# TensorE alternates the two layers of neighbouring expert turns, and GpSimd makes 21 more small gathers, in a graph and expert network kernel

## The chip, the cores and the metric

The kernel runs on one core of a Trainium2 chip. The metric is the device time of one execution in microseconds (us), lower is better. Before the change it is 1894.84 us, the median of three runs (1893.95 to 1897.71).

## The reference, cut to what matters

A layernorm of 6250 nodes x 256 features feeds a graph attention layer over 100,000 edges and a linear attention; their sum is the input of a mixture of experts. Only the last part bears on the change:

```python
logits = xt @ Wr + br                      # 8 experts
top_p, top_idx = jax.lax.top_k(softmax(logits), 2)
weights = top_p / top_p.sum(axis=-1, keepdims=True)
xn = (xt - mu) * jax.lax.rsqrt(var + LN_EPS)
xe = xn * ln_g[e] + ln_b[e]
h = gelu(xe @ W1[e] + b1[e])               # 256 -> 1024, exact gelu
y = h @ W2[e] + b2[e]                      # 1024 -> 256
out = x + sum over the two chosen experts of weight * y
```

## The kernel before

The program is written out by hand for each engine; semaphores order the engines against each other, and each engine works through its own queue in order. It has these stages: the table of node features; a walk over the edges in 196 groups of 512, for which GpSimd gathers rows of the table (784 indirect DMAs, line 843) while the two attention layers are finished beside it; the router, in which VectorE finds each token's two experts and its place; and the expert stage, which is the change's place.

In the expert stage the 12,500 pairs of token and expert are sorted into blocks of 128 rows, each block owned by one expert. There are 57 **turns**: 48 of two blocks (256 rows, "double" below) and 9 of one block (128 rows, "single"). `place_of` sets their order: three doubles, then nine times five doubles and a single, so the singles are turns 8, 14, 20 and so on to 56, the last. `subs_of(s)` is 1 for a single.

A turn `s` goes through the engines like this:

- GpSimd gathers the rows (`get_rows`, line 893) up to five turns ahead, and the gates (`get_gates`, line 898).
- TensorE transposes the rows (`pe_turn_rows`, line 2279); VectorE scales them (`dve_affine`, line 1932), ScalarE casts the high half and VectorE makes the low half (lines 1206 and 1937).
- TensorE computes the first layer, `pe_up` (line 2294): 8 parts `f` of six matmuls, each with a moving operand as wide as the turn has rows. The expert is a number in memory: `expert_at` (line 549) loads it into a register, and the addresses of the weights are worked out from it by register instructions between the matmuls, two `k` by two halves of the weights for a part.
- ScalarE takes the gelu of each two parts (`act_tile`, line 1183), VectorE splits it into two halves (lines 1951 and 1952).
- TensorE computes the second layer, `pe_down` (line 2315): 8 parts of six matmuls for a double and three for a single, all with a moving operand of 256 columns. It may start when VectorE has read the banks of the turn before (`y_ready`).
- VectorE adds the bias (`dve_answer`, line 1966), ScalarE multiplies by the gate (`act_gate`, line 1197), and GpSimd adds the block to the output (`add_rows`, line 907), one block after the other: each add waits until the one before it has landed.

TensorE's own order is in `pe_tile`: in turn `s` it transposes the rows of turn `s + 1`, then does the first layer of turn `s`, then the second layer of turn `s - 1`. VectorE's turn `s` (`dve_tile`) prepares the rows of `s + 1`, then splits the four pairs of parts of `s`, then answers for `s - 1`; the instructions of an engine run in that order.

When all is done, each engine ends with a DRAIN instruction and the program is over.

Of the kernel before, what the change touches and what calls it, by code (L numbers as in the profile page):

```python
# [9 lines left out]
P = 128  # L10
N, D = 6250, 256
# [24 lines left out]
FR = 2 * P  # L36
# [18 lines left out]
AHEAD, GATES_AHEAD = 5, 2  # L55
PARKS = 2 * (X + 1)
# [117 lines left out]
def build(nc, x, src, dst, gnn_w, attn_l, attn_r, gnn_bias, wq, bq, wk, bk, wv, bv, wo, bo,  # L174
          wr, br, ln_g, ln_b, w1, b1, w2, b2, out):
    ctx = ExitStack()
    with ctx:
        ctx.enter_context(nc.allow_non_contiguous_dma(reason="narrow rows of parameters"))

        def sb(name, shape, dt=F32):  # L180
            return ctx.enter_context(nc.sbuf_tensor(name, shape, dt))

        def sem(name):
            return ctx.enter_context(nc.semaphore(name))
# [165 lines left out]
        iota16 = sb("iota16", [P, P], F16)  # L350
        small = region(sb("small", [P, 488])[:, :], 488)
# [30 lines left out]
        tb_few = tables([P, X])  # L382
        wide = region(mid_g[:, :, :].rearrange("p a b -> p (a b)"), RG * D)
# [90 lines left out]
        consts = sem("consts")  # L474
        consts_v = sem("consts_v")
# [307 lines left out]
        def _(pool):  # L783
# [6 lines left out]
            pool.memset(ones16[:, :], 1.0).then_inc(consts, 1)  # L790
            pool.memset(edge_rows[:, 0:7, :], 0).then_inc(pads_set, 1)
# [140 lines left out]

            pool.wait_ge(places_ready, 1)
# [1045 lines left out]
        def _(pe):  # L1979
# [303 lines left out]
            def pe_up(s):  # L2283

                u, rows = s % 2, rows_at(s)
                e = expert_at(pe, s)
                pe.wait_ge(x_turn, 2 * s + 2)
                for f in range(KF):
                    if f % 2 == 0 and s:
                        pe.wait_ge(gelu_ready, 4 * s - 3 + f // 2)  # L2290
                    n = 0
                    for k in range(KD):
                        for wh, xh in ((0, 0), (0, 1), (1, 0)):
                            last = pe.matmul(bank[f // 2][:, (f % 2) * FR:(f % 2) * FR + rows],  # L2294
                                             w1_s[:, bass.ds(e, 1), k, wh, f * P:(f + 1) * P].rearrange("p a b -> p (a b)"),
                                             x_hl[:, u, xh, k, 0:rows], start=n == 0, stop=n == 5)
                            n += 1
                    if f % 2 == 1:
                        last.then_inc(h_made, 1)

            def pe_down(s):
                u = s % 2
                if s == 0:
                    pe.wait_ge(w2_in, X * 16)
                    pe.wait_ge(tau_turn, 1)
                e = expert_at(pe, s)
                if s:
                    pe.wait_ge(y_ready, s)
                for f in range(KF):
                    if f % 2 == 0:  # L2310
                        pe.wait_ge(h_turn, 8 * s + 2 + f)
                    for wh, hhs in ((0, (0, 1)), (1, (0,))):
                        for sub in range(subs_of(s)):
                            for hh in hhs:
                                last = pe.matmul(bank[4 + sub][:, 0:D], h_hl[:, u, hh, f, sub * P:(sub + 1) * P],  # L2315
                                                 w2_s[:, bass.ds(e, 1), f // (KF // 2), wh, f % (KF // 2), :].rearrange("p a b -> p (a b)"),
                                                 start=f == 0 and wh == 0 and hh == 0, stop=f == KF - 1 and wh == 1)
                last.then_inc(y_made, 1)
# [8 lines left out]
            def pe_tile(s):  # L2327
                if s + 1 < FT:
                    pe_turn_rows(s + 1)
                pe_up(s)  # L2330
                if s == 0:
                    pe_unused()
                else:
                    pe_down(s - 1)
# [35 lines left out]
```

## Time and profile before

| | us |
|---|---|
| median of three runs | 1894.84 |
| the profiled execution | 1891.82 |
| its span, first to last instruction | 1890.1 |
| TensorE busy | 1581.7 (84%) |
| VectorE busy | 1368.5 (72%) |
| GpSimd busy | 1218.3 (64%) |
| ScalarE busy | 1079.1 (57%) |

In the profile PE is TensorE's matmuls and PEld its weight loads, which overlap them; DVE is VectorE, ACT ScalarE, POOL GpSimd, SP SyncE. A name with q behind it (PEldq, POOLq) is the engine's instruction sequencer, which works out registers, waits on semaphores and hands work to the engine ahead of its execution. `L2294` is line 2294 of the kernel before. The start of a timeline row is in us from the span's start.

### The profile page before, as it was taken

Reading aid. Unit: us, or ns where it says so; the run is one execution under the profiler, and the core shown is the slowest. Engines: PE = TensorE matmul, PEld = TensorE weight load, DVE = VectorE, ACT = ScalarE, POOL = GpSimd, SP = SyncE. Lnnn points to the kernel's source line nnn. Section 1 sums busy time; section 2 is a strip of 40 time slices with the busy share of each in tenths; the row PEclk is TensorE's granted clock in tenths of the full one; section 3 lists DMA queues with packets and bytes.
Section 4 is the critical chain, followed back from the end, with each engine's and each line's share of the span. In section 5 each row is a group of like instructions: output and inputs, shape, how many; then the busy total and the mean of one; then the engine's idle time right before and its main releaser. Section 6 shows DMA issues by size and latency. Waiting matters only on the chain. (4 is left out here: it accounts for less than half of the span.)

```text
span 1890.1 us, 46784 instructions
## 1 busy us (share of the span) xinstructions
PE 1581.7 (84%) x11358; PEld 1300.0 (69%) x11358; DVE 1368.5 (72%) x3833; ACT 1079.1 (57%) x3043; POOL 1218.3 (64%) x1135
## 2 busy tenths in 40 slices
PE   7858777788787989888887778629999999999995
PEld 5635555455566777777775666517888889888884
DVE  6656567677667888888888999897666656665662
ACT  4655566566666666677666776563444444444441
POOL 2077777777777777777677776105666666666663
PEclk8978899999999999999998888658999999999998
DMA  7745565566544555555555665652333333333332
GB/s 223 247 122 138 168 174 164 165 176 179 150 117 127 155 150 150 141 152 145 142 139 179 183 202 162 200 199 45 53 48 53 49 48 50 53 50 49 46 53 24
DMA packets 149158, 239.37 MB, mean 127 GB/s; under 512 B 27536, under 2 KB 114824, under 8 KB 147624
## 3 DMA queue, kind: packets, MB, share of 16 engines
q0 software_dynamic: 61216, 132.39, 30.4%
q1 hardware_dynamic: 85944, 103.15, 16.8%
q8 instruction: 109, 1.79, 0.4%
q14 instruction: 145, 1.19, 0.2%
q10 hardware_dynamic: 1744, 0.85, 0.2%
HBM read 180.78 MB, written 55.52 MB: 125 GB/s over the span
## 5 line engine op out<-in xcount | busy, mean ns | idle before, releaser
L843 POOL DMA_INDIRECT w_s<-table,w_s x784 | 806.4, 1029 | 279.9 <-issue 231.4
L2092 PE MATMUL bank<-w_s 128*128 128x260 f32 x1952 | 515.9, 410 | 110.3 <-DVE w_s L1536 110.0
L2092 PEld LDWEIGHTS bank<-w_s 128*128 128x128 f32 x1952 | 378.1, 201 | 206.0 <-DVE w_s L1536 139.9
L1026 ACT ACTIVATE w_s<-w_s 128x64 f32 x976 | 260.3, 337 | 68.3 <-ACT w_s L1021 68.1
L1536 DVE SCALAR_TENSOR_TENSOR w_s<-w_s 128x256 f32<-128x256 f32 x732 | 275.7, 426 | 26.7 <-ACT w_s L1026 18.9
L2294 PE MATMUL bank<-acc,w_s 128*128 128x256 f16 (+1 forms) x2736 | 290.4, 265 | 1.6 <-DVE acc L1937 1.5
L2315 PE MATMUL bank<-w_s,acc 128*128 x2520 | 284.5, 273 | 7.2 <-DVE acc L1951 5.5
L907 POOL DMA_INDIRECT out<-mid_g,low_g x105 | 177.2, 1687 | 151.2 <-ACT mid_g L1197 90.6
L2294 PEld LDWEIGHTS bank<-acc,w_s 128*128 x2736 | 252.9, 98 | 30.7 <-issue 2.1
L2315 PEld LDWEIGHTS bank<-w_s,acc 128*128 128x128 f16 x2520 | 245.8, 98 | 37.0 <-issue 8.7
L1033 ACT COPY w_s<-bank 128x512 bf16<-128x512 bf16 x244 | 142.1, 582 | 202.8 <-PE bank L2072 202.3
L1197 ACT ACTIVATE mid_g<-acc 128x256 f32<-128x256 f32 x105 | 48.1, 501 | 276.2 <-DVE acc L1966 217.7
L1183 ACT ACTIVATE acc<-bank,params 128x256 f32<-128x256 f32 (+1 forms) x456 | 174.3, 459 | 31.1 <-PE bank L2294 22.7
L1503 DVE SCALAR_TENSOR_TENSOR w_s<-w_s,iota 128x512 bf16<-128x512 f32 x244 | 181.8, 745 | 1.9 <-issue 0.9
L893 POOL DMA_INDIRECT acc<-xn_d,low_g x105 | 102.6, 977 | 95.9 <-DVEq L1891 63.4
L1952 DVE SCALAR_TENSOR_TENSOR acc<-acc 128x512 f16<-128x512 f32 (+1 forms) x228 | 149.7, 656 | 7.8
L1522 DVE SCALAR_TENSOR_TENSOR w_s<-w_s 128x16 f32<-128x16 f32 x244 | 43.4, 178 | 151.4 <-POOLq L849 148.9
L1015 ACT CAST w_s<-w_s 128x512 f32<-128x512 bf16 x244 | 152.1, 624 | 0.0
L1966 DVE SCALAR_TENSOR_TENSOR acc<-bank,stage 128x256 f32<-128x256 f32 x105 | 40.1, 420 | 140.1 <-PE bank L2315 139.6
L898 POOL DMA_INDIRECT acc<-gate_d,low_g x105 | 111.6, 1063 | 32.0 <-issue 32.0
L2072 PE MATMUL bank<-w_s 128*128 128x128 bf16 x976 | 99.5, 227 | 38.7 <-DVE w_s L1503 37.9
L2072 PEld LDWEIGHTS bank<-w_s 128*128 128x128 bf16 x976 | 75.7, 104 | 79.2 <-DVE w_s L1503 37.4
(308 smaller groups left out, 2187.6 us busy)
## 6 DMA issues: line engine op xcount, KB each, us to landing
stage<-in_L_ffn_W SPq DMA_DIRECT2D x32, 512.0 KB, 4.2
w_s<-table,w_s POOLq DMA_INDIRECT x784
w_s<-in_x SPq DMA_DIRECT2D x48, 256.0 KB, 4.0
w_s<-xT_d SPq DMA_DIRECT2D x96, 128.0 KB
w_park<-low_g SPq DMA_DIRECT2D x18, 512.0 KB
w_s<-w_park SPq DMA_DIRECT2D x9, 1024.0 KB, 9.1
xn_d<-acc SPq DMA_DIRECT2D x7, 896.0 KB, 5.0
table<-w_s SPq DMA_DIRECT2D x24, 260.0 KB, 3.5
```

What stands on the lines that cost most here:

```text
L843: pool.indirect_dma_start(out=ring[:, u, k, :], out_offset=None, in_=table[:, :], in_offset=bass.IndirectOffsetOnAxis(ap=srcT[:, (q * RING ...
L907: pool.indirect_dma_start(out=out[:, :], out_offset=bass.IndirectOffsetOnAxis(ap=add_at[:, column(s, sub):column(s, sub) + 1], axis=0), in ...
L1015: act.copy(hot32[:, k.at % 4, :, :], hot16[:, k.at % 4, :, :]).then_inc(hot32_ready, 1)
L1026: last = act.activation(m[:, e, 0:GD], rows[:, e, 0:GD], ACT.Copy, scale=m[:, e, GD:HC])
L1183: last = act.activation(h32[:, f, 0:n], bank[q][:, (f % 2) * FR:(f % 2) * FR + n], ACT.Gelu, bias=b1T[:, bass.ds(e * KF + f, 1)], scale=UN ...
L1503: dve.scalar_tensor_tensor(hot16[:, k.at % 4, :, :], dstT[:, bass.ds(group * SUB, SUB)].unsqueeze(2).to_broadcast([P, SUB, P]), tile_v[:, ...
L1536: last = dve.scalar_tensor_tensor(m[:, e:e + GH, 0:GD], rows[:, e:e + GH, 0:GD], 1.0, m[:, e:e + GH, GD:HC].to_broadcast([P, GH, GD]), ALU ...
L1952: lambda: dve.scalar_tensor_tensor(h_hl[:, u, 1, f0:f1, 0:n], h32[:, f0:f1, 0:n], ASCALE, h_hl[:, u, 0, f0:f1, 0:n], ALU.mult, ALU.subtract))
L2072: last = pe.transpose(turned16[:, s, :], hot16[:, k.at % 4, s, :], ident16[:, :])
L2092: last = pe.matmul(bank[2 + k.at % 2][:, 0:ROW], hot32[:, k.at % 4, s, :], msg[:, k.at % 2, s, :], start=s == 0, stop=s == SUB - 1)
L2294: last = pe.matmul(bank[f // 2][:, (f % 2) * FR:(f % 2) * FR + rows], w1_s[:, bass.ds(e, 1), k, wh, f * P:(f + 1) * P].rearrange("p a b -> ...
L2315: last = pe.matmul(bank[4 + sub][:, 0:D], h_hl[:, u, hh, f, sub * P:(sub + 1) * P], w2_s[:, bass.ds(e, 1), f // (KF // 2), wh, f % (KF // ...
```

## The change

In a turn of 128 rows TensorE no longer does the first layer of `s` and then the second layer of `s - 1`: it alternates one part of the one with one part of the other (`pe_mixed`). The waits and the load of the expert of both stand at its start. `up_begin` and `down_begin`, which other turns use too, wait first and then load the expert; before, the load came first.

The second part adds `FILL` = 21 indirect gathers on GpSimd, each of 128 rows of 8 numbers from the router's weights at index 0, into a tile that nothing reads. They come after the last addition of the router stage and before the first gather of the expert stage. With the 784 gathers of the walk and 3 x 105 of the expert stage they make 1120, a multiple of 32.

```diff
+LOT = 32
+FILL = -(EC + 3 * COLS) % LOT
...
+        fill_at = sb("fill_at", [P, 1], I32)
...
+        filled = tables([P, FILL, X])
...
+            pool.memset(fill_at[:, :], 0).then_inc(fill_set, 1)
...
+            pool.wait_ge(fill_set, 1)
+            for n in range(FILL):
+                pool.indirect_dma_start(out=filled[:, n, :], out_offset=None, in_=wr[:, :],
+                                        in_offset=bass.IndirectOffsetOnAxis(ap=fill_at[:, :], axis=0)).then_inc(filled_up, 16)
+            pool.wait_ge(filled_up, 16 * FILL)
             pool.wait_ge(places_ready, 1)
...
+            def up_begin(s):
+                pe.wait_ge(x_turn, 2 * s + 2)
+                return expert_at(pe, s)
...
+            def down_begin(s):
                 if s == 0:
                     pe.wait_ge(w2_in, X * 16)
                     pe.wait_ge(tau_turn, 1)
-                e = expert_at(pe, s)
                 if s:
                     pe.wait_ge(y_ready, s)
+                return expert_at(pe, s)
...
+            def pe_mixed(s):
+
+                e_up, e_down = up_begin(s), down_begin(s - 1)
+                for f in range(KF):
+                    up_part(s, e_up, f)
+                    down_part(s - 1, e_down, f)
...
             def pe_tile(s):
                 if s + 1 < FT:
                     pe_turn_rows(s + 1)
-                pe_up(s)
-                if s == 0:
-                    pe_unused()
+                if subs_of(s) == 1:
+                    pe_mixed(s)
                 else:
-                    pe_down(s - 1)
+                    pe_up(s)
+                    if s == 0:
+                        pe_unused()
+                    else:
+                        pe_down(s - 1)
```

`up_part` and `down_part` are the bodies of the loops over `f` of `pe_up` and `pe_down`, unchanged, with their waits on `gelu_ready` and `h_turn`.

TensorE's queue at the start of a single turn, turn 8, in the kernel before (`ISA` is a register instruction, or one of the load's; the bank and tile names lack their numbers; waits stand in brackets):

```order
L2279 MATMUL bank<-ident,acc 128x128 [waits x_turn,rows_got1]
L2279 MATMUL bank<-ident,acc 128x128 x3
L549 TENSOR_LOAD low_g
L549 ISA x2
L2294 ISA [waits gelu_ready,x_turn]
L2294 MATMUL bank<-acc,w_s 128x128 x2
L2294 ISA
L2294 MATMUL bank<-acc,w_s 128x128
```

and the same place now, where line 2290 is the transposes, 554 the load, 2306 the first layer and 2328 the second:

```order
L2290 MATMUL bank<-ident,acc 128x128 [waits x_turn,rows_got1]
L2290 MATMUL bank<-ident,acc 128x128 x3
L554 TENSOR_LOAD low_g [waits x_turn]
L554 ISA x2
L554 TENSOR_LOAD low_g [waits y_ready]
L554 ISA x2
L2306 ISA [waits gelu_ready]
L2306 MATMUL bank<-acc,w_s 128x128 x2
L2306 ISA
L2306 MATMUL bank<-acc,w_s 128x128
```

The wait on `y_ready`, which stood behind the 48 matmuls of the first layer, stands ahead of them now, and the second layer's load of the expert stands behind that wait. The first layer keeps its matmuls and its register instructions; the second layer's come between its parts.

GpSimd's queue at the start of the expert stage before:

```order
L887 TENSOR_TENSOR acc<-acc,w_s 128x7x256 [waits mid_read0,x2_made,elu_made]
L893 DMA acc<-xn_d,low_g 128x256 [waits xn2_out0,xn2_out1,places_ready]
L893 DMA acc<-xn_d,low_g 128x256 x3
```

and now:

```order
L893 TENSOR_TENSOR acc<-acc,w_s 128x7x256 [waits mid_read0,x2_made,elu_made]
L941 DMA low_g<-in_L_ffn_Wr,fill_at 128x8 [waits fill_set]
L941 DMA low_g<-in_L_ffn_Wr,fill_at 128x8 x20
L899 DMA acc<-xn_d,low_g 128x256 [waits xn2_out1,xn2_out0,places_ready,filled_up]
```

The 21 gathers stand between the last addition and the wait on `places_ready`; nothing else of GpSimd's moves.

## Rows read from the trace of the kernel before

**Rows 1.** The page: TensorE's granted clock in 40 slices of the span, in tenths.

```profile
PEclk8978899999999999999998888658999999999998
```

**Rows 2.** Groups by line, 1280 to 1890 us: line, engine, operation, shapes, count | busy, mean ns | idle before, releaser.

```profile
L2315 PE MATMUL bank<-w_s,acc 128*128 x2520 | 284.5, 273 | 7.2 <-DVE acc L1951 5.5 <-DVE acc L1966 1.1 <-issue 0.6
```

**Rows 3.** Timeline of TensorE, end of turn 7, turn 8: start us, us, what [idle before].

```profile
1361.22 5.40 PE L2315 MATMUL bank<-w_s,acc 128*128 x48
1366.46 0.60 PE L2279 MATMUL bank<-ident,acc 128*128 128x128 f32 x4
1366.90 3.28 PE L2294 MATMUL bank<-acc,w_s 128*128 128x128 f16 x48
1370.89 5.41 PE L2315 MATMUL bank<-w_s,acc 128*128 x48 [0.70 <-DVE acc L1951]
1376.13 0.60 PE L2279 MATMUL bank<-ident,acc 128*128 128x128 f32 x4
```

**Rows 4.** Lines 2294 and 549, turn 8: duration ns min/median/max, first and last start.

```profile
L2294 PE MATMUL bank<-acc,w_s x48: 219/219/228, 1366.9 to 1370.0; 128*128 128x128 f16 x48
L2294 PEldq FUSED_REGOPS  x32: 46/46/46, 1365.7 to 1369.9; - x32
...
L549 PEldq TENSOR_LOAD <-low_g x1: 299/299/299, 1370.0 to 1370.0; - x1
```

**Rows 5.** Timeline of VectorE at the start of turn 8.

```profile
1366.79 0.76 DVE L1966 SCALAR_TENSOR_TENSOR acc<-bank,stage 128x256 f32<-128x256 f32 x2 [2.78 <-PE bank L2315]
```

**Rows 6.** Timeline of the last turn and the end.

```profile
1857.37 3.19 PE L2294 MATMUL bank<-acc,w_s 128*128 128x128 f16 x48
1857.69 0.76 DVE L1966 SCALAR_TENSOR_TENSOR acc<-bank,stage 128x256 f32<-128x256 f32 x2 [2.62 <-PE bank L2315]
1858.59 0.91 ACT L1197 ACTIVATE mid_g<-acc 128x256 f32<-128x256 f32 x2 [5.32 <-DVE acc L1966]
1859.44 2.17 ACT L1183 ACTIVATE acc<-bank,params 128x128 f32<-128x128 f32 x8
1860.36 1.58 POOL L907 DMA_INDIRECT out<-mid_g,low_g  x1 [4.38 <-ACT mid_g L1197]
1861.21 5.41 PE L2315 MATMUL bank<-w_s,acc 128*128 x48 [0.65 <-DVE acc L1951]
1862.10 0.29 DVE L1951 TENSOR_SCALAR acc<-acc 128x256 f16<-128x256 f32 x1
1862.42 0.43 DVE L1952 SCALAR_TENSOR_TENSOR acc<-acc 128x256 f16<-128x256 f32 x1
...
1866.78 0.76 DVE L1966 SCALAR_TENSOR_TENSOR acc<-bank,stage 128x256 f32<-128x256 f32 x2 [3.94 <-PE bank L2315]
1869.57 1.56 POOL L907 DMA_INDIRECT out<-mid_g,low_g  x1 [3.01 <-DMA out<-mid_g,low_g]
...
1878.57 1.56 POOL L907 DMA_INDIRECT out<-mid_g,low_g  x1 [2.91 <-issue]
```

**Rows 7.** GpSimd's DRAIN instructions, at the end (L177) and at the start (L2360).

```profile
L177 POOLq DRAIN  x1: 7462/7462/7462, 1882.4 to 1882.4; - x1
...
L2360 POOLq DRAIN  x1: 171/171/171, 0.4 to 0.4; - x1
```

**Rows 8.** Timeline of GpSimd from the router stage on.

```profile
1205.70 3.96 POOL L887 TENSOR_TENSOR acc<-acc,w_s 128x1792 f32<-128x1792 f32 x1 [11.89 <-DVE acc L1693]
1273.05 1.19 POOL L893 DMA_INDIRECT acc<-xn_d,low_g  x1 [63.39 <-DVEq L1891]
1274.54 0.94 POOL L893 DMA_INDIRECT acc<-xn_d,low_g  x1 [0.30 <-issue]
```

**Rows 9.** VectorE beside GpSimd: one operation of the router, and line 1536 in the walk.

```profile
1205.94 3.78 DVE L1741 SCALAR_TENSOR_TENSOR small<-small 128x35 f32<-128x35 f32 x1
...
L1536 DVE SCALAR_TENSOR_TENSOR w_s<-w_s x721: 410/420/481, 109.4 to 1179.7; 128x256 f32<-128x256 f32 x181
```

**Rows 10.** Timeline of TensorE: the first layer of turn 0.

```profile
1282.58 7.35 PE L2294 MATMUL bank<-acc,w_s 128*128 128x256 f16 x48 [1.50 <-DVE acc L1937]
```

More of the change, by code:

```diff
@@ L474, in build @@
         consts = sem("consts")
+        fill_set, filled_up = sem("fill_set"), sem("filled_up")
         consts_v = sem("consts_v")
@@ L2281, in pe_turn_rows, with up_part @@
                 last.then_inc(rows_turned, 1)
-            def pe_up(s):
+            def up_begin(s):
+                pe.wait_ge(x_turn, 2 * s + 2)
+                return expert_at(pe, s)
+            def up_part(s, e, f):
                 u, rows = s % 2, rows_at(s)
-                e = expert_at(pe, s)
[L2287 to L2302, printed above, removed]
+                if f % 2 == 0 and s:
+                    pe.wait_ge(gelu_ready, 4 * s - 3 + f // 2)
+                n = 0
+                for k in range(KD):
+                    for wh, xh in ((0, 0), (0, 1), (1, 0)):
+                        last = pe.matmul(bank[f // 2][:, (f % 2) * FR:(f % 2) * FR + rows],
+                                         w1_s[:, bass.ds(e, 1), k, wh, f * P:(f + 1) * P].rearrange("p a b -> p (a b)"),
+                                         x_hl[:, u, xh, k, 0:rows], start=n == 0, stop=n == 5)
+                        n += 1
+                if f % 2 == 1:
+                    last.then_inc(h_made, 1)
+            def down_begin(s):
                 if s == 0:
@@ L2305, in pe_down, with down_part, pe_up @@
                     pe.wait_ge(tau_turn, 1)
-                e = expert_at(pe, s)
                 if s:
                     pe.wait_ge(y_ready, s)
-                for f in range(KF):
[L2310 to L2318, printed above, removed]
+                return expert_at(pe, s)
+            def down_part(s, e, f):
+                u = s % 2
+                if f % 2 == 0:
+                    pe.wait_ge(h_turn, 8 * s + 2 + f)
+                for wh, hhs in ((0, (0, 1)), (1, (0,))):
+                    for sub in range(subs_of(s)):
+                        for hh in hhs:
+                            last = pe.matmul(bank[4 + sub][:, 0:D], h_hl[:, u, hh, f, sub * P:(sub + 1) * P],
+                                             w2_s[:, bass.ds(e, 1), f // (KF // 2), wh, f % (KF // 2), :].rearrange("p a b -> p (a b)"),
+                                             start=f == 0 and wh == 0 and hh == 0, stop=f == KF - 1 and wh == 1)
+                if f == KF - 1:
+                    last.then_inc(y_made, 1)
+            def pe_up(s):
+                e = up_begin(s)
+                for f in range(KF):
+                    up_part(s, e, f)
+            def pe_down(s):
+                e = down_begin(s)
+                for f in range(KF):
+                    down_part(s, e, f)
+            def pe_mixed(s):
+                e_up, e_down = up_begin(s), down_begin(s - 1)
+                for f in range(KF):
+                    up_part(s, e_up, f)
+                    down_part(s - 1, e_down, f)
             def pe_unused():
```

## The prediction

> **What bounds the kernel now.** I read the page first, then the expert stage by lines, then TensorE's timeline turn by turn, and last the end of the program.
>
> The page shows TensorE at nine tenths or more through the last quarter of the span, at the full granted clock, 2.4 GHz [rows 1]. Grouped by lines, 1280 to 1890 us, the second layer's matmuls have 284.5 us busy and only 7.2 us idle ahead of them [rows 2]. So the expert stage is as long as TensorE's work, and its few gaps are worth looking at one by one. They lie in the single turns. In turn 8 [rows 3] the second layer runs 48 matmuls of 256 columns from 1370.89 to 1376.13, 5.24 us, 0.109 us each, the pace of every double turn (1361.22 to 1366.46). The first layer, 48 matmuls of 128 columns, should take half of that, 2.6 us. It starts at 1366.90 and the second layer starts at 1370.89, so 3.99 us go by. That is 1.4 us too much, and all of it in front of the second layer.
>
> The sequencer's rows say why [rows 4]. Its 32 register instructions for the first layer run from 1365.7 to 1369.9, 0.13 us apiece, 4.2 us for all. They are the same number for a part of 128 columns and for one of 256. In a double turn the matmuls need 5.24 us and hide them; in a single one the work handed ahead is used up, and TensorE goes at the sequencer's pace. Then comes the load of the second layer's expert, starting at 1370.0; the first matmul behind it runs at 1370.89, 0.9 us later. The "DVE acc L1951" that [rows 3] name as releaser is not what ended this gap: it belongs to turn 8's own gelu, and the second layer of turn 7 doesn't wait on it.
>
> The end is bound otherwise. The last blocks are added to the output one after the other: adds start at 1869.57 and 1878.57 with one between, 4.5 us each [rows 6]. Then GpSimd's DRAIN takes 7.46 us, while all other engines are through [rows 7].
>
> **The mixed turns.** Alternating keeps every matmul and every register instruction. What goes is the sequencer's shortfall: 32 steps of the first layer and 16 of the second at 0.13 us are 6.2 us, against 2.65 + 5.24 = 7.9 us of matmuls. Only the first part, which has nothing in front of it, still runs at the sequencer's pace, 0.2 us more than its matmuls. So a mixed double pair should take 8.1 us where it takes 9.23 (1366.90 to 1376.13): 1.1 us gained a turn, 9.9 for nine, if TensorE could start at once.
>
> It can't. The wait on `y_ready` now stands ahead of the first layer, and so does the load behind it. `y_ready` is VectorE's answer for the turn whose second layer ended as this turn began: in turn 8 it runs from 1366.79 for 0.76 us, so to 1367.55 [rows 5]. Before, 48 matmuls lay between and hid it. The load and the first register steps took 0.9 us from the start of the load to a matmul [rows 4]; one semaphore instruction less stands in them now, so I take 0.8. The first matmul runs at 1368.35 instead of 1366.90, and the turn ends at 1368.35 + 8.1 = 1376.45 instead of 1376.13: 0.3 us later. For eight turns that is **+2.6 us**. The bounds: without the wait at the start -1.1 each; with a 1.5 us gap and a first layer that still takes 3.99 us, +1.5 each.
>
> Behind the waiting sequencer stand only this turn's matmuls. ScalarE and VectorE get the parts of the single turn later and farther apart; ScalarE is idle for 5.3 us before its gates [rows 6] and VectorE for 2.8 us before its answer [rows 5], and the next turn's second layer comes 5 us later, so I cost that at nothing. Should the cover go, it costs what VectorE is late, at most 1 us a turn. In the double turns "wait, then load" costs nothing: there the sequencer is ahead, and `y_ready` is old when it gets there.
>
> **The last turn, 56, costs more** [rows 6]. It has no transposes, so TensorE waits from 1857.37 to 1857.69 + 0.76 + 0.8 = 1859.25; with 8.1 us the second layer of turn 55 ends at 1867.35, before at 1861.21 + 5.24 = 1866.45. And its answer now comes behind VectorE's split of turn 56's last pair, whose first layer ends only at 1866.7. With two gelus of 0.27 us (2.17 for eight), splits of 0.29 and 0.43 and some 0.4 us of handing over, that is 1868.4, and 0.2 for the expert's load; answer 0.76, 0.1, gate 0.91 as in ACT's row: 1870.4. From the end of a gate (1858.59 + 0.91 = 1859.50) to the add at 1860.36 is 0.86 us. So the add that starts at 1869.57 starts at 1871.3: **+1.7 us**, and the two behind follow it. Bounds: +0.2, if only TensorE's 0.9 us counts and the add has its slack, and +2.5.
>
> **The 21 gathers.** GpSimd is idle for 63.4 us between its last addition and the first gather of the expert stage [rows 8]. A gather comes every 1.25 us (1273.05 with 1.19 busy, next at 1274.54; the usual step is 0.94 + 0.30), so 21 take 26 us plus a landing. The work that hides them is the router on VectorE; were that cover gone they would cost these 26 us. Nothing reads the tile. The memset and the waits: nothing.
>
> Beside them runs VectorE, whose chain is the critical one there. At 1205.94 an operation of 35 columns took 3.78 us while GpSimd's addition of 3.96 us ran [rows 8, 9]: a lock between the two exists in this kernel. But 721 operations of line 1536, two inputs in SBUF each, ran beside the walk's 784 gathers and took 410/420/481 ns [rows 9]. The most a gather adds by that is 61 ns, 1.3 us for 21; the median adds none, and I take 0. The Trainium skill speaks against the change here: "SBUF — State Buffer", SBUF: two separate sides, has the shared port pair as an exclusive lock which whoever starts first holds for the whole instruction. Applied to gathers, that would make the sum some 20 us larger; it is a rival below.
>
> **What the gathers may change is the DRAIN.** At the start, with no DMA issued, it took 0.17 us; at the end, after 1099 indirect DMAs, 7.46 [rows 7], and no row shows a transfer in it. So it is GpSimd's own work on what its DMAs left behind. What was issued in all can't be the measure alone, at 6.6 ns a DMA; what is left of a lot would be. 1099 is 34 lots of 32 and 11 more; with 1120 nothing is left over. Whether that is the rule no row shows. The bounds: down to the 0.17 of the start, -7.3; unchanged, 0; and if a full lot were left where 11 were, 7.3 x 32/11 = 21, +14. I take an end near the short DRAIN, 0.5 us, **-7.0**, because of the two lengths that the trace has, long with a remainder and short with nothing outstanding, the changed count is nearer to the second.
>
> **Sum.** -7.0 + 2.6 + 1.7 = -2.7 us against the profiled execution's 1891.82 (span 1890.1 and 1.7 around it). The median of the runs shown is 3.0 us above that execution; I carry the difference over: 1894.84 - 2.7 = 1892.1. A measurement of this kernel can tell about 0.2%, 3.8 us, from no change, so this is no change that can be told.
>
> **The rivals.**
> 1. *The DRAIN doesn't care, and the kernel is slower.* If its length has nothing to do with lots of 32, the wait on `y_ready` at the head of nine turns is what remains: +4.3, 1899.1. It decides when the DRAIN stays above 6.7 us. For it: no row links the DRAIN to a count. Against: nothing else explains 7.46 us without a transfer.
> 2. *The DRAIN falls by a part only*, say half, because it has a fixed share: -3.6 + 4.3, 1895.5.
> 3. *Alternating pays as meant*: the wait is not late, or the first layer gains more. By [rows 4] -1.1 a turn and -7.0: 1894.84 - 9.9 - 7.0 = 1877.9. Against: the answer ends 0.65 us after the transposes [rows 3, 5], and in turn 56 it comes as late [rows 6].
> 4. *The clock falls.* The gap at the head of a mixed turn, 1.5 us and 1.9 in the last, is the longest that TensorE has in this stage. In turn 0, behind such waiting, 48 matmuls took 7.35 us instead of 5.40 before the clock was up [rows 10]. At 1.95 us a turn, nine turns are 17.6: 1909.7. Against: the gaps of 0.7 us left it at full [rows 1, 3], and 8 us of matmuls follow each.
> 5. *VectorE is locked by each gather*: 21 x 0.94 = 19.7 us on the router's chain, 1911.8. Against it are the 721 operations of [rows 9]. This is what the Trainium skill's page above would make of it.
>
> **How the numbers follow.** Forecast 0.43, rival 1 0.26, rival 2 0.12, rival 3 0.09, rival 4 0.06, rival 5 0.04. The forecast's own spread is 2 us either way (the last turn's bounds, and 0.2 us on each of eight waits), and the runs' another 1. Faster than 1891.05 are rival 3 and a third of the forecast: 0.24. Slower than 1898.63 are rivals 4 and 5, 0.6 of rival 1 and a little of rival 2: 0.27. The rest is 0.49. The range takes in the forecast with its spread, rivals 1 and 2 and some of 3's side: 1887 to 1902. The forecast alone would be 1889 to 1895.
>
> **What would show it.** In turn 8 the transposes end, TensorE is idle for 1.4 to 1.5 us with VectorE's L1966 row ending inside that gap, then first and second layer alternate for 8.1 us, and the single turn takes 9.9 to 10.0 us from transposes to transposes instead of 9.67. GpSimd's last DRAIN is below 1 us. The 21 gathers end before 1245 and the first gather of the expert stage starts within 1 us of 1273. A single turn of 8.6 us, a DRAIN of 7.4 us, an expert stage that starts 20 us late, or a granted clock below full between 1300 and 1860 would each prove me wrong, as rivals 3, 1, 5 and 4 have it.

## The result, and the profile after

The change makes the kernel slower by 0.31%: 1901.22 us median (1895.98 to 1907.75, 18 runs) against 1896.11 us for the kernel before beside it (1891.4 to 1901.12, 18 runs), ratio 1.0031, 95% interval 1.0021 to 1.0041. Forecast were 1892.1 us and no change that can be told; the range, 1887 to 1902, holds the time. Rival 1, "the DRAIN doesn't care", said 1899.1. Some executions of two kernels below (one of nine of e9, two of twelve of e13) ran in a slower state; the ratios leave these out and the medians don't.

| profiled executions | before | after |
|---|---|---|
| the execution, us | 1891.82 | 1898.09 |
| its span | 1890.1 | 1896.4 |
| first transposes of the expert stage start at | 1277.40 | 1277.66 |
| turn 0, transposes to transposes of turn 1 and on | 12.77 | 13.44 |
| turns 1 to 7 | 76.30 | 76.23 |
| turns 8 to 54 | 480.20 | 483.37 |
| the eight single turns in them, mean | 9.62 | 10.01 |
| start of turn 55 to GpSimd's last DRAIN (the tail) | 35.73 | 38.00 |
| that DRAIN | 7.46 | 7.46 |

From here on, the length of a turn `s` is the time from TensorE's transposes in it to those in the next. A tail is good to 0.05 us, because the start of a DRAIN is printed to a tenth. The 6.3 us between the two spans are 3.2 in turns 8 to 54, of which the eight single turns are 3.1 (8 x 0.39), 2.3 in the tail, 0.7 in turn 0 and 0.3 before the stage. Nothing came back.

In the new numbering line 2290 is the transposes, 554 the load of the expert, 2306 the first layer, 2328 the second, 1948 the low half of the rows, 1977 the answer, 1208 the gate, 913 the add and 941 the new gathers. The clock, on the page of after, answers to [rows 1]:

```profile
PEclk8978899899999999999998888659999999999998
```

It stayed up through the expert stage. Groups by line, 1280 to 1897 us, as [rows 2]:

```profile
L2306 PE MATMUL bank<-acc,w_s 128*128 128x256 f16 (+1 forms) x2736 | 298.3, 265 | 14.2 <-DVE acc L1977 12.0 <-DVE acc L1948 2.2
L2328 PE MATMUL bank<-w_s,acc 128*128 x2520 | 296.5, 274 | 2.9 <-DVE acc L1977 2.9
```

The idle time has moved from the second layer (7.2 before, now 2.9) to the first (1.6 before, now 14.2), and all but 2.2 us of it waits for VectorE's answer. The higher busy time of the two groups is no sign of more work: the matmuls are the same, and where the parts alternate, the modelled end of a row lies behind the start of the next (1369.20 + 0.60 and 1369.70 below). Turn 8 on TensorE's timeline, to set beside [rows 3]:

```profile
1367.33 0.60 PE L2290 MATMUL bank<-ident,acc 128*128 128x128 f32 x4
1369.20 0.60 PE L2306 MATMUL bank<-acc,w_s 128*128 128x128 f16 x6 [1.26 <-DVE acc L1977]
1369.70 0.83 PE L2328 MATMUL bank<-w_s,acc 128*128 x6
1370.36 0.50 PE L2306 MATMUL bank<-acc,w_s 128*128 128x128 f16 x6
...
1376.64 0.82 PE L2328 MATMUL bank<-w_s,acc 128*128 x6
1377.29 0.60 PE L2290 MATMUL bank<-ident,acc 128*128 128x128 f32 x4
```

VectorE's timeline has the answer that ends the wait, and line 554's rows the two loads; the second start, 1368.4, is right behind it:

```profile
1367.66 0.75 DVE L1977 SCALAR_TENSOR_TENSOR acc<-bank,stage 128x256 f32<-128x256 f32 x2 [2.77 <-PE bank L2328]
```

```profile
L554 PEldq TENSOR_LOAD <-low_g x2: 298/302/307, 1365.8 to 1368.4; - x2
```

The mixed part takes 1369.20 to 1377.29 = 8.09 us, no shortfall of the sequencer left in it, and the gap ahead of it takes away what that gave: the transposes take 0.44 us (1366.46 to 1366.90 in [rows 3]), so TensorE is idle from 1367.77 to 1369.20, 1.43 us.

Turn 0 on TensorE's timeline (its first layer, [rows 10] before) and on VectorE's:

```profile
1280.28 1.09 PE L2290 MATMUL bank<-ident,acc 128*128 128x128 f32 x4 [1.53 <-DMA acc<-xn_d,low_g]
1283.52 7.34 PE L2306 MATMUL bank<-acc,w_s 128*128 128x256 f16 x48 [2.16 <-DVE acc L1948]
```

```profile
1282.03 0.69 DVE L1948 TENSOR_TENSOR acc<-acc 128x512 f16<-128x512 f32 x1 [0.74 <-ACT acc L1217]
```

From the start of that low half to the first matmul it is 1.49 us; before, 1281.74 to 1282.58, it was 0.84. The last turn and the end, as [rows 6]:

```profile
1861.72 0.76 DVE L1977 SCALAR_TENSOR_TENSOR acc<-bank,stage 128x256 f32<-128x256 f32 x2 [2.61 <-PE bank L2328]
...
1863.30 0.60 PE L2306 MATMUL bank<-acc,w_s 128*128 128x128 f16 x6 [1.74 <-DVE acc L1977]
...
1872.02 0.43 DVE L1963 SCALAR_TENSOR_TENSOR acc<-acc 128x256 f16<-128x256 f32 x1
1872.86 0.76 DVE L1977 SCALAR_TENSOR_TENSOR acc<-bank,stage 128x256 f32<-128x256 f32 x2 [0.41 <-issue]
1873.76 0.91 ACT L1208 ACTIVATE mid_g<-acc 128x256 f32<-128x256 f32 x2 [2.10 <-DVE acc L1977]
...
1875.49 1.56 POOL L913 DMA_INDIRECT out<-mid_g,low_g  x1 [4.90 <-ACT mid_g L1208]
...
1880.10 1.55 POOL L913 DMA_INDIRECT out<-mid_g,low_g  x1 [3.05 <-DMA out<-mid_g,low_g]
1884.66 1.56 POOL L913 DMA_INDIRECT out<-mid_g,low_g  x1 [3.01 <-DMA out<-mid_g,low_g]
```

The answer for turn 55 is now behind VectorE's last split (line 1963). Then GpSimd: its last DRAIN, which answers to [rows 7], and its timeline with the gathers, to [rows 8].

```profile
L179 POOLq DRAIN  x1: 7462/7462/7462, 1888.7 to 1888.7; - x1
```

```profile
1205.71 3.96 POOL L893 TENSOR_TENSOR acc<-acc,w_s 128x1792 f32<-128x1792 f32 x1 [6.78 <-DVE acc L1704]
1209.84 1.19 POOL L941 DMA_INDIRECT low_g<-in_L_ffn_Wr,fill_at  x1 [0.17 <-issue]
...
1235.39 0.95 POOL L941 DMA_INDIRECT low_g<-in_L_ffn_Wr,fill_at  x1 [0.30 <-issue]
1273.58 0.94 POOL L899 DMA_INDIRECT acc<-xn_d,low_g  x1 [37.24 <-DVEq L1902]
```

The DRAIN has the same 7462 ns after 1120 indirect DMAs as after 1099. The gathers fit the idle time with 37 us to spare.

### The profile page after: what moved, and what is told of

It reads as the page before. It is cut to its first block, busy times and chain, and to the rows that moved or that the text cites. A ratio compares the mean times of both kernels' runs of the same rounds, so it can differ in the third digit from the quotient of the medians.

```text
span 1896.4 us, 46695 instructions
## 1 busy us (share of the span) xinstructions
PE 1582.0 (83%) x11358; PEld 1302.1 (69%) x11358; DVE 1371.0 (72%) x3833; ACT 1080.4 (57%) x3043; POOL 1247.2 (66%) x1157
## 4 chain that ended last, share of the span: by engine, by line
PE 42%; POOL 18%; issue 15%; DVE 10%; ACT 6%; DMA 6%; ACTq 2%; DVEq 1%; POOLq 1%; SPq 0%
POOL w_s L849 18%; PE bank L2306 15%; PE bank L2328 14%; PE bank L2103 5%; DMA w_s<-table,w_s 4%; PE bank L2176 2%; ACT w_s L1037 2%; ACT w_s L1064 1%; DVE w_s L1547 1%; PE bank L2290 1%; PE bank L2155 1%; ACTq L1018 1%; PE bank L2020 1%; PE bank L2151 1%; DVE acc L1854 1%
## 5 line engine op out<-in xcount | busy, mean ns | idle before, releaser
L2306 PE MATMUL bank<-acc,w_s 128*128 128x256 f16 (+1 forms) x2736 | 298.3, 265 | 14.2 <-DVE acc L1977 12.0
L2328 PE MATMUL bank<-w_s,acc 128*128 x2520 | 296.5, 274 | 2.9 <-DVE acc L1977 2.9
L2306 PEld LDWEIGHTS bank<-acc,w_s 128*128 x2736 | 256.5, 98 | 45.3 <-issue 16.7
L913 POOL DMA_INDIRECT out<-mid_g,low_g x105 | 181.2, 1725 | 150.9 <-ACT mid_g L1208 102.4
L1962 DVE TENSOR_SCALAR acc<-acc 128x512 f16<-128x512 f32 (+1 forms) x228 | 97.9, 430 | 56.9 <-ACT acc L1194 56.8
## 6 DMA issues: line engine op xcount, KB each, us to landing
w_s<-w_park SPq DMA_DIRECT2D x9, 1024.0 KB, 11.2
xn_d<-acc SPq DMA_DIRECT2D x7, 896.0 KB, 10.5
```

The costliest lines, as they stand in the source:

```text
L913: pool.indirect_dma_start(out=out[:, :], out_offset=bass.IndirectOffsetOnAxis(ap=add_at[:, column(s, sub):column(s, sub) + 1], axis=0), in ...
```

## The experiments

The total scatters by 10 us from run to run, since the walk over the edges does: its last gather starts anywhere between 1179 and 1191 us. So each experiment is read in two ways, by its ratio and by the stage lengths of its trace. The runs e5, e6, e7, e13 and e14 were timed where the kernel before itself takes 2270 to 2275 us, because the walk is longer there (the first transposes come at 1655 to 1688 us); their totals scatter by 20 to 40 us. Call them the long series. The expert stage isn't quite the same in it either: each of its five traces has two to five double turns of 11.2 to 17.4 us instead of 10.9, in some of which TensorE waits for nothing that the profile shows, and the traces of the other series have none, except for e8's many DRAINs. e13 and e15 are one kernel, and their turns 8 to 54 take 482.9 and 471.8 us. So from the long series the single turns and the DRAIN are used, and the tail with care; its ratios are given too.

### Each part alone: e1 and e2

e1 is the kernel after without the 21 gathers, e2 the kernel before with them:

```diff
 e1, from after
-            for n in range(FILL):
-                pool.indirect_dma_start(out=filled[:, n, :], ...)
 e2, from before
+            for n in range(FILL):
+                pool.indirect_dma_start(out=filled[:, n, :], ...)
```

> The changed kernel without the 21 gathers, alternation kept. Theory A (all of the loss is TensorE waiting at the head of turns, the gathers do nothing): as the changed kernel, ratio to the kernel before 1.002 to 1.004; GpSimd's last DRAIN stays at 7.46 us with 1099 indirect DMAs as with 1120; single turns of 10.0 us. Theory B (the gathers lie on a path or disturb the router stage): back at the kernel before, ratio 0.999 to 1.001. Theory C (the DRAIN's length depends on the count, and 7.46 us twice was chance): another length of DRAIN than 7.46 us.

> The kernel before with the 21 gathers alone. Theory A: same time as before, ratio 0.999 to 1.001, DRAIN 7.46 us, first gather of the expert stage within 1 us of 1273. Theory B: slower by most of the 6 us, ratio 1.002 to 1.004.

| | ratio to before | single turns | tail | DRAIN | last addition to first transposes |
|---|---|---|---|---|---|
| before | | 9.62 | 35.73 | 7.462 | 71.70 |
| after | 1.0031 (1.0021 to 1.0041) | 10.01 | 38.00 | 7.462 | 71.95 |
| e1 | 1.0040 (1.0025 to 1.0054) | 10.01 | 37.92 | 7.462 | 71.66 |
| e2 | 0.9995 (0.9984 to 1.0007) | 9.62 | 36.13 | 7.462 | 72.02 |

The loss belongs to the order on TensorE; the gathers alone make no difference that can be told. They cost 0.3 us between GpSimd's last addition and the first transposes: 71.95 and 72.02 with them (and 71.89, 72.04 in e3, e4), 71.70 and 71.66 without. They don't touch the DRAIN.

In the long series that stretch is far longer with them: 88.4 us in e6 and in e7, which have the gathers, against 71.7, 71.6 and 71.7 in e5, e13 and e14, which don't. VectorE's operations beside the gathers keep their length (0.45 us for 280 columns in e7 as in after); what is new is one wait, for TensorE's last logits. It is this row in after, and the second one in e7:

```profile
1223.28 0.27 DVE L1776 TENSOR_TENSOR w_s<-bank,w_s 128x112 f32<-128x112 f32 x1 [0.88 <-PE bank L2235]
```

```profile
1614.03 0.28 DVE L1776 TENSOR_TENSOR w_s<-bank,w_s 128x112 f32<-128x112 f32 x1 [17.38 <-remote]
```

In e7 the logits' matmuls end at 1597.8 by the profile, so it is the signal that came late. Meanwhile 12 of ScalarE's semaphore instructions took 0.7 us each instead of 0.04. e6 and e7 are one execution each, so it isn't shown beyond doubt that the gathers do this, nor why in one series and not in the other.

### The order on TensorE: e3, e4, e6

e3 puts each load back ahead of its wait. e4 moves, besides, three of the first layer's parts ahead of the wait on `y_ready`; e6 moves one.

```diff
 e3, from after
             def up_begin(s):
+                e = expert_at(pe, s)
                 pe.wait_ge(x_turn, 2 * s + 2)
-                return expert_at(pe, s)
+                return e
 (and the same in down_begin)
 e4, from e3; in e6 LEAD_PARTS is 1
-                e_up, e_down = up_begin(s), down_begin(s - 1)
-                for f in range(KF):
+                e_up = up_begin(s)
+                e_down = expert_at(pe, s - 1)
+                for f in range(LEAD_PARTS):
                     up_part(s, e_up, f)
+                pe.wait_ge(y_ready, s - 1)
+                for f in range(KF):
                     down_part(s - 1, e_down, f)
+                    if f + LEAD_PARTS < KF:
+                        up_part(s, e_up, f + LEAD_PARTS)
```

> The changed kernel with the load of the expert ahead of each wait, as the kernel before had it; the wait on y_ready still at the head of the mixed turns. Theory A: the gap at the head of a mixed turn falls from 1.43 to 0.9 us and the turn from 10.0 to 9.45, turn 0 gets back its 0.65 us (13.44 to 12.8), the last turn 0.5: 5.5 us less than the changed kernel, ratio to the kernel before 0.999 to 1.001. Theory D (alternating itself is slow, by switching of weights or banks): single turns stay at 10.0.

> As e3_loads_first, and three parts of the first layer run ahead of the wait on y_ready, then the layers alternate, so the second layer's last three parts stand alone. Theory A: the wait is covered, the gap at the head is gone and a single turn takes 8.6 us (0.44 of transposes, 7.9 of matmuls, 0.3 lost) against 9.62 in the kernel before: 8.0 us in eight turns; the last turn gives nothing at the end, since the adds behind it are 4.5 us apart and bound by the one before. 1888 us, ratio to the kernel before 0.995 to 0.997. Theory D: 9.6 or more a turn, no gain.

> As e4_three_ahead with one part ahead instead of three. Theory A: one part is 0.34 us of matmuls against some 0.65 us until the answer ends and 0.2 until a matmul, so a gap of 0.3 to 0.5 us remains and the single turn takes 8.9 to 9.1 us, between 9.34 with none ahead and 8.61 with three. Were the gap not the wait on y_ready, the number of parts ahead would not matter: 8.6.

| | ratio to before | single turns | tail |
|---|---|---|---|
| e3, loads first | 0.9992 (0.9977 to 1.0006) | 9.34 | 37.37 |
| e6, and one part ahead | (one execution) | 8.81 | 36.59 |
| e4, and three parts ahead | 0.9957 (0.9942 to 0.9971) | 8.61 | 36.19 |

TensorE's timeline in turn 8 of e3, and of e4:

```profile
1373.39 0.60 PE L2290 MATMUL bank<-ident,acc 128*128 128x128 f32 x4
1374.61 0.62 PE L2307 MATMUL bank<-acc,w_s 128*128 128x128 f16 x6 [0.62 <-DVE acc L1977]
```

```profile
1373.39 0.60 PE L2291 MATMUL bank<-ident,acc 128*128 128x128 f32 x4
1373.83 1.25 PE L2308 MATMUL bank<-acc,w_s 128*128 128x128 f16 x18
1375.09 0.83 PE L2331 MATMUL bank<-w_s,acc 128*128 x6
...
1380.05 2.13 PE L2331 MATMUL bank<-w_s,acc 128*128 x18
1382.01 0.60 PE L2291 MATMUL bank<-ident,acc 128*128 128x128 f32 x4
```

So of the turn's 10.01 us the load behind the wait is 0.67 and the wait itself 0.73: with 18 matmuls of work in front of it nobody waits, no gap is left, and the turn takes 8.61. One part in front takes off 0.53 of the 0.73, and the turn of 8.81 us is a little shorter than the 8.9 to 9.1 expected. The matmuls alone are 0.44 + 2.6 + 5.24 = 8.3 us. e4's order is worth 1.0 us a turn against the kernel before, near the 1.1 that the prediction worked out for alternating; the change spent it, and 0.4 more, on where it put one wait and one load. How much of the 1.0 is alternating isn't shown: e4 also has the second layer's load at the head of the turn, where in the kernel before it stood in the gap of 0.70 us ahead of the second layer [rows 3, 4], and the old order with that load moved alone was not run.

### The last turn: e7 and e5

e7 is after with the old order in the last turn alone. e5 is e4 with the old order there and without the gathers.

```diff
-                if subs_of(s) == 1:
+                if subs_of(s) == 1 and s + 1 < FT:
                     pe_mixed(s)
```

> The changed kernel with the last turn (56) in the old order, turns 8 to 50 as changed. Theory A: eight single turns stay at 10.0 us, and from the transposes of turn 55 to GpSimd's DRAIN it takes 35.7 to 36.1 us as in the kernel before instead of 38.0. Rival: the tail is long by the single turns before it or by the DMA landings, and stays at 38.

> Three parts ahead as in e4_three_ahead, without the 21 gathers, and the last turn in the old order. Theory A: eight turns of 8.6 us are all that counts, so the same time as e4_three_ahead within 0.1%: 1887 us, ratio to the kernel before 0.995 to 0.997. If the last turn's alternation or the gathers cost anything once the wait is covered, it is under 1 us.

e7: tail 36.13 instead of 38.00, single turns 10.03, DRAIN 7.46. So 1.9 us of the tail's 2.3 are the last turn's order. e5: single turns 8.59, tail 36.04, as e4's 36.19, but ratio 1.0013 (0.9977 to 1.0049), where 0.995 to 0.997 was expected: a miss. Its turns 41 and 47 take 13.97 and 17.41 us, 9.5 us more than e4's, and the long series has no trace of the kernel before to tell whether that one has such turns too. So the gain in the total is shown only where the kernel before takes 1896 us. With three parts ahead it makes no difference which order the last turn has, and that e4's gain in the single turns isn't the gathers' doing is seen here and in e9.

### What the DRAIN is: three small kernels

They copy `x` to `out` and leave out everything else of the computation; beside the copy GpSimd issues 0, 1 or 43 of the small gathers and waits for them.

```diff
-GATHERS = 43
+GATHERS = 0      (and 1)
```

> The same small kernel with no gather at all (all of the computation is left out). Lots or counts: a DRAIN near the 0.17 us of the program's start. Fixed: 7.46 us.

> The same small kernel with one gather (all of the computation is left out). Lots: short, or a little over the kernel without any. A fixed price for having used GpSimd's DMAs at all: 7.46 us here and near 0.2 with none. Fixed whatever the program does: 7.46 us in both.

> A kernel of nothing but a copy of x to the output and, on GpSimd, 43 gathers of 128 rows of 8 numbers (all of the computation is left out). 43 is 32 and 11 more, the remainder that 1099 has. If the DRAIN at the end counts what is left of a lot, or what was issued, it takes another time than with 0 and 1 gathers; if it is a fixed piece of the program's end, 7.46 us with any count.

GpSimd's DRAIN at the end takes 41 ns after none, 133 ns after one, and after 43:

```profile
L13 POOLq DRAIN  x1: 3572/3572/3572, 73.8 to 73.8; - x1
```

(3572 - 133) / 42 = 82 ns for each indirect DMA, though all had landed. At this price 7462 ns are (7462 - 41) / 82 = 90 DMAs. The real kernels have ten times as many and their DRAIN is the same to the nanosecond for 1099 and 1120, so there is a ceiling, and no lots of 32. That it lies at 90 is worked out from the price, not measured: no run has a count between 52 and 784. And every indirect DMA here has 128 indices, so a price per DMA and one per index can't be told apart.

### Working it off earlier: e8 and e9

e9 is e4 without the gathers. e8 is e9 with a DRAIN at 58 places of GpSimd's queue:

```diff
                 if late >= 0:
+                    pool.drain()
                     pool.wait_ge(y_gated, late + 1)
...
+            pool.drain()
             pool.wait_ge(places_ready, 1)
```

> This kernel has three parts of the first layer ahead of the wait on y_ready in every single turn, no gathers, and an explicit DRAIN on GpSimd's queue at two places: ahead of the wait for the router's places (in 63 us of idle time) and ahead of each turn's wait for the gated answer. Theory A: the DRAIN's 7.46 us is work on what the last 90 or so indirect DMAs left, 82 ns each, and it can be done earlier, where GpSimd is idle. Then the DRAIN in the router's idle time takes about 7.4 us, each turn's DRAIN covers some 6 DMAs and takes about 0.5 us, and GpSimd's last DRAIN falls from 7.46 us to at most 0.5 us. If the adds at the end keep their distance, the whole is 7 us shorter than the twin without DRAINs (e9), about 1880 us on a chip where the kernel before takes 1896, ratio to it 0.991 to 0.993. Theory B: the last DRAIN is a fixed sum that an earlier one does not touch: last DRAIN 7.46 us, total as e9. Theory C: the DRAIN at each turn's head must also wait until the DMAs in flight have landed, so that the gathers are issued late and the adds move apart: transposes of turn 55 to the last DRAIN longer than 36.2 us by 1 us or more, or single turns longer than 8.6 us.

> The twin of e8 without the explicit DRAINs: three parts of the first layer ahead of the wait on y_ready in all nine single turns, no gathers. Expected as e4, less at most 0.3 us for the gathers: single turns 8.6 us, transposes of turn 55 to the last DRAIN 36.2 us, last DRAIN 7.46 us, ratio to the kernel before 0.995 to 0.997 on a chip where that takes about 1896 us. If the gathers had anything to do with what e4 gained (rival), this one is at 1.000.

e9: 1888.48 us, ratio 0.9955 (0.9937 to 0.9973), single turns 8.54, tail 36.14. e8: 1964.03 us, ratio 1.0344 (1.032 to 1.0369). Its DRAINs: line 926 is the one in each turn, 940 the router's, 180 the last:

```profile
L926 POOLq DRAIN  x57: 1187/5706/8372, 1304.2 to 1954.6; - x57
```

```profile
L940 POOLq DRAIN  x1: 8671/8671/8671, 1214.0 to 1214.0; - x1
```

```profile
L180 POOLq DRAIN  x1: 128/128/128, 1963.4 to 1963.4; - x1
```

Two of the three things expected held at once. The last DRAIN fell from 7.46 to 0.13 us, so this is work that can be done earlier. But a turn's DRAIN takes 5.7 us and not 0.5: there were some six DMAs since the last one, 0.5 us at 82 ns, and the rest it waited for the add and the gathers issued just before. In turns 1 to 3 it ends 0.28 us after the last of them has landed. The one ahead of the last add, with two adds since the one before it, took 4.2 us; the step from add to add is 4.6. GpSimd had no room for that in every turn, and single turns went to 11.4 us. In the router's idle time it cost nothing: 71.64 us from the last addition to the first transposes, as without it. Its own 8.67 us, where 7.4 was expected, begin with that addition of 3.97 us, so how much of them is work on the DMAs can't be read.

### One or two DRAINs: e10 to e15

All are e9 (e11: the kernel before) with `pool.drain()` ahead of that wait in chosen turns:

```diff
+                if late == FT - 4:        (e10, e11: turn 53)
+                if late == FT - 12:       (e12: turn 45)
+                if late == FT - 7:        (e14: turn 50)
+                if late in (FT - 7, FT - 1):   (e13, e15: turns 50 and 56)
+                    pool.drain()
                     pool.wait_ge(y_gated, late + 1)
```

> e9's kernel with one explicit DRAIN on GpSimd's queue, ahead of turn 53's wait for the gated answer, four turns before the end. Theory A, each indirect DMA leaves 82 ns of work for the next DRAIN, up to about 90 DMAs: 10 DMAs follow it, so the last DRAIN takes 41 + 10 x 82 = 0.9 us instead of 7.46. The early one takes 6 to 8.5 us and makes turn 53's adds up to 3 us late; the chain of adds has that room before turn 55. So transposes of turn 55 to the last DRAIN 36.2 to 37, the whole 6 to 6.6 us below e9, ratio to the kernel before 0.991 to 0.993. Theory B, whatever follows a DRAIN brings its whole sum back: last DRAIN 7.46 us, total as e9 (0.9955) or more. Theory C, the late adds of turn 53 run on into the chain: last DRAIN 0.9 us, but transposes of turn 55 to the last DRAIN longer by 3 us, so 0.9935 to 0.995.

> The kernel before with the same single DRAIN ahead of turn 53's wait for the gated answer and nothing else changed. Theory A: last DRAIN 0.9 us instead of 7.46, single turns 9.62 as before, transposes of turn 55 to the last DRAIN 35.7 to 36.6, ratio 0.996 to 0.998. This is the gain of 7.0 us that the prediction expected of the 21 gathers. Theory B: 7.46 us and ratio 1.000.

> As e10, but the one DRAIN is ahead of turn 45's wait for the gated answer. 52 indirect DMAs follow it (22 adds, 18 gathers of gates, 12 of rows). Theory A: last DRAIN 41 + 52 x 82 ns = 4.3 us. Theory B: 7.46 us. Rival to A's linear form, the cost is that of rings or lots: some other step between 0.9 and 7.46.

> e9's kernel with two explicit DRAINs on GpSimd's queue: ahead of turn 50's and of turn 56's wait for the gated answer. By 82 ns per DMA: one DMA follows the second, so the last DRAIN is 0.13 us. If e10's 1.8 us were turn 53's adds running on into the chain, they are made up for here, since three more turns lie between: transposes of turn 55 to the last DRAIN 36.1 and 0.3 more for the second DRAIN (e8's last step between adds was 4.84 us instead of 4.57), 36.5. Whole 7.0 us below e9: about 1881 where the kernel before takes 1896, ratio 0.990 to 0.993. Rival: any early DRAIN costs the tail some 2 us (tail 38), ratio 0.994.

> The same with the DRAIN of turn 50 alone. 24 DMAs follow it: last DRAIN 41 + 24 x 82 = 2.0 us; transposes of turn 55 to the last DRAIN 36.1 to 36.4; whole 5.3 us below e9, ratio 0.991 to 0.994. Rival as above: tail 38, ratio 0.995.

> e13's kernel once more, timed where the kernel before takes about 1895 us. From e13's trace: single turns 8.6 us, transposes of turn 55 to the last DRAIN 37.4 us, last DRAIN 0.13 us. Against the kernel before that is 8 single turns x 1.05 = 8.4 us, the tail 1.7 us longer, the DRAIN 7.3 us shorter and turn 0 up to 0.6 longer: 13 us, ratio 0.992 to 0.994. If the DRAINs give nothing in the total, it is at e9's 0.9955 or above.

| | DMAs behind the last explicit DRAIN | last DRAIN, ns (41 + n x 82) | tail | median us, ratio to before |
|---|---|---|---|---|
| e9 | | 7462 | 36.14 | 1888.48, 0.9955 (0.9937 to 0.9973) |
| e10 | 10 | 863 (861) | 37.96 | 1883.4, 0.9942 (0.9929 to 0.9954) |
| e11 | 10 | 863 (861) | 38.44 | 1889.39, 0.9981 (0.9967 to 0.9995) |
| e12 | 52 | 4293 (4305) | 36.30 | 1879.28, one execution |
| e14 | 24 | 2007 (2009) | 36.74 | 2273.07, 0.9999 (0.9969 to 1.0029) |
| e13 | 1 | 128 (123) | 37.43 | 2267.98, 0.997 (0.9937 to 1.0002) |
| e15, e13's kernel | 1 | 128 (123) | 38.39 | 1880.49, 0.9915 (0.9902 to 0.9927) |

The rows of e10's last DRAIN, of e12's early one and of e12's last one; the two last ones were forecast from the price per DMA:

```profile
L180 POOLq DRAIN  x1: 863/863/863, 1879.4 to 1879.4; - x1
```

```profile
L926 POOLq DRAIN  x1: 9204/9204/9204, 1751.8 to 1751.8; - x1
```

```profile
L180 POOLq DRAIN  x1: 4293/4293/4293, 1873.1 to 1873.1; - x1
```

The price is exact to 12 ns over 1 to 52 DMAs. e11 shows its worth by itself: the kernel before, with this one instruction more, is faster by 0.19% (0.05 to 0.33), 3.6 us. By its trace the last DRAIN gives 6.6 us and the tail, 2.7 us longer, takes back much of it; the 7.0 us that the gathers were forecast to bring are not reached this way either.

What the last DRAIN gives isn't all kept. The early one lasts 8.5 to 10.5 us, since it works off 90 DMAs and also waits for the add in flight, and makes the adds behind it late; they catch up slowly, because two adds of 4.6 us are already 9.2 of a turn of 10.9. Against e9, turn 55's first add comes 1.8 us later in e10, four turns ahead of the end; 1.2 in e15, seven ahead; 0.1 in e12, twelve ahead. That is the expected theory C, at less than its 3 us. e13 and e14, also seven ahead, show 0.1 and 0.7, but in them turns 53 and 54 together are 2.7 and 5.4 us longer than two usual ones, which lets the adds catch up. Their ratios, 0.9999 and 0.997, lie above the 0.991 to 0.994 and 0.990 to 0.993 expected, with their whole intervals: in the long series no gain of the DRAINs can be told. A second loss, which the 0.3 us expected for the second DRAIN had too small, is seen in GpSimd's last two adds in e15:

```profile
1869.70 1.55 POOL L913 DMA_INDIRECT out<-mid_g,low_g  x1 [2.92 <-DMA out<-mid_g,low_g]
1875.36 1.56 POOL L913 DMA_INDIRECT out<-mid_g,low_g  x1 [4.11 <-issue]
```

Their step is 5.66 us instead of 4.6: the DRAIN there takes 5044 ns with 23 DMAs to work off, where e8's at the same place took 4218 with two. Still e15 beats both kernels, ratio 0.9915, the lowest of all. By its trace it has 8 x 1.06 = 8.5 us from the single turns and 7.3 from the DRAIN, less 2.7 in the tail and 0.4 in turn 0, 12.7 in all; the ratio says 16 (14 to 19). Where the other 3 us (1 to 6) come from stays open.

## Why the prediction was wrong

**The DRAIN, the step that failed.** "What the gathers may change is the DRAIN", -7.0 us; measured 0. Its two ends were rightly read from [rows 7], and so was that it is GpSimd's own work on what its DMAs left behind: it is, 82 ns each. The wrong turn is the sentence "What was issued in all can't be the measure alone, at 6.6 ns a DMA; what is left of a lot would be". A count with a ceiling has the same two ends, and there the 21 further DMAs change nothing. The lot of 32 came from the change's own constant, not from a row; the prediction says itself that no row shows the rule, and still gave it 0.43 against rival 1's 0.26. With 0 in that place the sum would have been +4.3, 1899.1, as rival 1 has it. That the stated range holds the measured time is owed to its taking in rival 1: the forecast alone, 1889 to 1895, doesn't.

**The mixed turns, right in mechanism.** In turn 8 the gap was 1.43 us (forecast 1.45), from the answer's end to the first matmul 0.79 (0.8), the mixed part 8.09 (8.1), the turn 0.29 us longer (0.3). All eight came to +3.1 instead of +2.6, because turn 8 isn't their mean: it took 9.67 before where the mean was 9.62, and 9.96 after where it was 10.01. e3 and e4 bear out the cause, the wait and the load behind it.

**The double turns, and turn 0 where it wasn't looked for.** "In the double turns 'wait, then load' costs nothing" held for turns 1 to 7 (76.23 against 76.30) and failed in turn 0, where TensorE really waits for `x_turn`: the load of 0.65 us now stands behind it. It is there in both kernels with this order, 1.49 us from the start of the low half to the first matmul in after and in e1, and in none with the load ahead: 0.84, 0.84 and 0.83 in before, e2 and e9, and 0.93 and 0.96 in e3 and e4. The prediction read [rows 10] for the clock and priced the edit at nothing. The length of turn 0 as a whole says less: it is 12.2 to 13.4 us in kernels with the same order, and the clock comes up in it sooner or later: the granted clock is 0.79 from 1282.4 to 1290 us in e11 (12.2 us) and 0.66 from 1283.4 to 1291 us in e9 (13.4 us).

**The last turn**: +2.3 instead of +1.7, with e7 at 1.9. The gap was 1.91 (1.88), and the first add of turn 55 came 1.9 us later, reckoned from the transposes (22.90 before, 24.79 after), where 1.7 was forecast. The other 0.4 is in the steps from that add to the DRAIN, 0.2 between the adds and 0.2 behind them, which differ that much between executions (e2's tail is 36.13 with before's order).

**The gathers**: 0.3 us instead of 0, below the 1.3 us of 61 ns a gather [rows 9], where the kernel before takes 1896 us; in the long series the two traces with them are 16.7 us longer there, by a late signal that the prediction has nowhere.

**The rivals.** 1 came true. 3, "alternating pays as meant", fell for this order; its gain in the turns, though not its 7.0 us of the DRAIN, is what e4 has. 4 fell: the clock stayed up behind gaps of 1.43 us; it fell only for the last 24 matmuls, behind a wait of 2.9 us (granted clock 0.66 from 1874 to 1879 us, 1.00 from 1863 to 1872), and their answer was ready before the chain of adds wanted it. 5 fell, and with it what the Trainium skill would give here: "SBUF — State Buffer", SBUF: two separate sides, has the pair of ports shared by VectorE and GpSimd as an exclusive lock for a whole instruction. It would be 20 us for 21 gathers; after and e2 to e4 show 0.3. The 16.7 us of e6 and e7 come near its price and are not its mechanism: VectorE's operations beside the gathers keep their lengths there, and one wait has all of it. That an operation of 35 columns took 3.78 us beside an addition of GpSimd's is in [rows 9]; no operation beside the gathers was lengthened like that.

## What to carry to other kernels

Ahead of a wait that is satisfied late, put the loads and the work that don't need it: here 18 matmuls and the two loads turned a loss of 0.4 us a turn into a gain of 1.0. When an instruction at the end of a program takes long and no row says why, a small kernel that varies the count of its suspected cause decides what two rows can't. If GpSimd issues indirect DMAs, look at its last DRAIN: one placed earlier, where GpSimd is idle and its adds have room, takes the time off the end. And a "free" filler isn't free everywhere: with the same 21 gathers the router stage was 0.3 us longer in one series and 16.7 in another.

## What was not expected of the hardware

- GpSimd's DRAIN costs 41 ns and 82 ns for each indirect DMA (of 128 indices) since the last DRAIN, even when all have landed, up to 7462 ns (90 DMAs, an estimate from the price). A DRAIN with a DMA in flight also waits for that (4.2 us behind one add).
- The indirect adds have almost no slack in the double turns, 9.2 of 10.9 us, so that a DRAIN of 9.0 us still makes an add 1.2 us late five turns on (e15, turn 50 to turn 55).
- The load of a register from SBUF ahead of a TensorE matmul is 0.65 us where the sequencer has waited just before, and nothing where it runs ahead.
- The same program took 1896 us in some series and 2270 in others, nearly all of the difference in the stage that gathers edges. The chip alone isn't shown to be the cause: under one chip number the kernel before took 2270 us beside e5 and, minutes later, 1899 us. In the long series single turns had the same lengths (8.6 us in e5 and e4), and a few double turns were up to 6.5 us longer.
